# Layer-0 quantised network of a fused transformer kernel: bias by TensorE, gelu out of PSUM, scaling of the inner values on ScalarE, x updated in place

## The reference, cut to what matters

```python
def _layernorm(x, axis=-1, eps=1e-05):
    m = jnp.mean(x, axis=axis, keepdims=True)
    v = jnp.var(x, axis=axis, keepdims=True)
    return (x - m) / jnp.sqrt(v + eps)

def rmsnorm(x):
    return x * jax.lax.rsqrt(jnp.mean(x * x, axis=-1, keepdims=True) + EPS)
def act_quant(x):
    scale = 127.0 / jnp.clip(jnp.max(jnp.abs(x), axis=-1, keepdims=True), 1e-05)
    q = jnp.clip(jnp.round(x * scale), -128.0, 127.0) / scale
    return x + jax.lax.stop_gradient(q - x)
def weight_quant(w):
    scale = 1.0 / jnp.clip(jnp.mean(jnp.abs(w)), 1e-05)
    q = jnp.clip(jnp.round(w * scale), -1.0, 1.0) / scale
    return w + jax.lax.stop_gradient(q - w)
def bitlinear(x, w, b):
    xq = act_quant(rmsnorm(x))
    wq = weight_quant(w)
    return jnp.einsum('bsd,fd->bsf', xq, wq) + b

h = bitlinear(x, w1, b1)                      # 128 -> 512
h = jax.nn.gelu(h, approximate=False)
return bitlinear(h, w2, b2)                   # 512 -> 128
...
x = x + _L0_ffn_ref(_layernorm(x, axis=-1), L0_ffn_w1, L0_ffn_b1, L0_ffn_w2, L0_ffn_b2)
```

## Time and profile before

| what | us |
|---|---|
| median of 3 runs (lowest, highest) | 3688.69 (3678.2, 3689.1) |
| the profiled execution's own time | 3686.95 |
| its span in the profile | 3685.4 |
| start of the phase in the span (first weight load issued) | 188.62 |
| start of the next phase in the span | 494.41 |

### The profile page before, as it was taken

How to read it: one execution, slowest core, us unless ns; L and a number is a source line. 1 busy time by engine, 2 the same in 40 slices (tenths; PEclk the granted TensorE clock), 3 DMA queues, 4 the chain that set the end, 5 groups by cost and what they waited for, 6 DMA issues and landing times. The chain is left out here.

```text
span 3685.4 us, 67574 instructions
## 1 busy us (share of the span) xinstructions
PE 2706.8 (73%) x24298; PEld 1883.8 (51%) x24298; DVE 2401.7 (65%) x5736; ACT 1075.1 (29%) x1536; POOL 578.2 (16%) x1018
## 2 busy tenths in 40 slices
PE   5823359995999999999966677789850666886256
PEld 4612236663666565656545555556530554664126
DVE  6789969993455555555444688867013557988668
ACT  4533357761000000000022244445310112443230
POOL 0012210000000000000000144324133002443003
PEclk9955579997999999999977888889975777998669
DMA  2010011102221212121100000010221220000001
GB/s 82 23 55 0 0 33 30 27 13 92 92 78 61 91 48 92 46 92 46 46 25 18 8 1 0 0 37 27 89 65 38 60 60 11 0 0 7 0 0 46
DMA packets 119643, 141.77 MB, mean 38 GB/s; under 512 B 75745, under 2 KB 87649, under 8 KB 118498
## 3 DMA queue, kind: packets, MB, share of 16 engines
q1 hardware_dynamic: 112002, 119.85, 10.6%
q0 software_dynamic: 7520, 20.34, 1.9%
HBM read 122.85 MB, written 17.30 MB: 38 GB/s over the span
## 5 line engine op out<-in xcount | busy, mean ns | idle before, releaser
L1387 PE MATMUL banks<-l1f_xe,l1f_w 128*128 128x512 f32 x1024 | 486.2, 597 | 10.5 <-DVE l1f_xe L1586 10.5
L1586 DVE TENSOR_TENSOR l1f_xe<-l1f_hT,l1f_rwb 128x512 f32<-128x512 f32 x256 | 173.3, 692 | 300.3 <-PE banks L1389 278.1
L1389 PEld LDWEIGHTS banks<-l1f_w,l1f_xe 128*128 128x128 f32 x2048 | 270.0, 192 | 123.6 <-issue 123.6
L1592 DVE TENSOR_TENSOR l1f_ae<-l1f_aoT,l1f_rwb 128x512 f32<-128x512 f32 x256 | 172.7, 690 | 160.7 <-PE banks L1417 156.1
L1389 PE MATMUL banks<-l1f_w,l1f_xe 128*128 128x128 f32 x2048 | 270.7, 275 | 0.0
L1387 PEld LDWEIGHTS banks<-l1f_xe,l1f_w 128*128 128x128 f32 x1024 | 176.7, 192 | 140.9 <-issue 126.5
L1417 PE MATMUL banks<-l1f_ae,l1f_w 128*128 128x512 f32 x512 | 225.4, 599 | 1.4 <-DVE l1f_ae L1592 1.4
L214 POOL COPY x<-xn 128x512 f32 (+1 forms) x32 | 19.6, 611 | 986.4 <-DVE xn L1616 973.0
L223 PE MATMUL banks<-consts,l3p_h 128*128 128x128 f32 x64 | 17.8, 434 | 200.1 <-DVE l3p_h L140 200.1
L1417 PEld LDWEIGHTS banks<-l1f_ae,l1f_w 128*128 128x128 f32 x512 | 97.1, 192 | 118.3 <-issue 116.1
L612 PE MATMUL banks<-identb,l0f_q 128*128 128x128 bf16 x256 | 30.2, 312 | 129.0 <-DVE l0f_q L536 129.0
(11 more groups left out here) (471 smaller groups left out, 6651.1 us busy)
## 6 DMA issues: line engine op xcount, KB each, us to landing
l1f_rwb<-l1f_shares SPq DMA_DIRECT2D x128, 512.0 KB, 4.3
l1a_ctx<-in_ctxT SPq DMA_DIRECT2D x32, 256.0 KB, 3.7
l3p_ctx<-in_ctxT SPq DMA_DIRECT2D x32, 256.0 KB, 4.0
l0a_ctxT<-in_ctxT SPq DMA_DIRECT2D x16, 256.0 KB, 2.7
l2f_sent<-l0f_zero SPq DMA_DIRECT2D x4, 1024.0 KB, 7.8
l2p_ctxT<-in_ctxT SPq DMA_DIRECT2D x16, 256.0 KB, 2.7
...
```

The lines of the kernel that those rows point to most:

```text
L1387: pe.matmul(bank, w[:, n, e, :], xe[:, e % NB, :], start=(e == 0), stop=(e == E - 1))
L1389: last = pe.matmul(v_bank[:, D * j:D * j + D], xe[:, e % NB, P * j:P * j + P], w[:, 2, e, :], start=(e == 0 and j == 0), stop=(e == E - 1) ...
L1586: dve.tensor_tensor(xe[:, e % NB, :], hT[:, m, :], rwb[:, m, e, :], ALU.mult).then_inc(s.xe_ready, 1)
L1592: dve.tensor_tensor(ae[:, e % NB, :], aoT[:, m, :], rwb[:, m, e, :], ALU.mult).then_inc(s.ae_ready, 1)
```

## The change

`b1` is no longer spread over 128 partitions. It lies in four partitions, zero but for one row for each tile, and PE adds it: after the product of a tile, a second matmul with 4 rows of contraction, in f32, accumulates into the same bank. Its left side is `back`, the inverse of the token's step, transposed by PE (L589) and copied out by ACT (L631). So the bank holds (product + b1/step), and ACT's gelu reads each bank out of PSUM with the token's step as its scale, tile by tile. DVE's `bias` is gone. The multiplication of the inner values by the token's scale is four ACT Copies with a scale (`scale`). The clip to -128..127 is gone in both quantisations, so rounding writes bf16 itself. `new_x` adds in place into `k.x`, to which POOL has added b2 before (`add_bias`); `k.xb`, `k.xn` and the copy back are not used. The buffers of `h2` and of the small values have four places instead of two, and the loop body has four steps.

```diff
-def quantise_rows(dve, chain, q, h, scal, mean):
-
-
-    amax, r, inv, rec = scal[:, 0, :], scal[:, 1, :], scal[:, INV, :], scal[:, 6, :]
-    chain.wait(chain.did(dve.tensor_tensor(amax, amax, r, ALU.mult)))
-    chain.wait(chain.did(dve.tensor_scalar(amax, amax, 1e-5, None, ALU.max)))
-    chain.did(dve.tensor_scalar(inv, amax, mean, 1.0 / 127.0, ALU.mult, ALU.mult))
-    chain.wait(chain.did(dve.reciprocal(rec, amax)))
-    chain.wait(chain.did(dve.tensor_scalar(rec, rec, 127.0, None, ALU.mult)))
-    for j in range(TG):
-        n = chain.did(dve.tensor_scalar(h[:, j, :], h[:, j, :], r[:, j:j + 1], rec[:, j:j + 1], ALU.mult, ALU.mult))
-    chain.wait(n)
-    chain.wait(chain.did(dve.tensor_scalar(h, h, ROUND, ROUND, ALU.add, ALU.subtract)))
-    return dve.tensor_scalar(q, h, 127.0, -128.0, ALU.min, ALU.max)
...
+    RING4 = 4
...
-        b1 = sb("b1", [P, F0])
+        b1 = sb("b1", [TG, TG, F0])
...
+        hq = sb("hq", [P, TG, D])
+        sx = sb("sx", [P, RING4, 6, TG])
+        sh = sb("sh", [P, RING4, 8, TG])
...
+        back = sb("back", [TG, 2, P])
+        h2 = sb("h2", [P, RING4, TG, F0])
...
+        back_psum = ps[4][0:TG, GT // 2:GT // 2 + P]
+        AMAX, R, STEP, LEVELS, BACK, MEAN, POWER, FACTOR = range(8)
...
+            sp.wait_ge(s.cleared, 1)
+            for j in range(TG):
+                sp.dma_start(b1[j:j + 1, j, :], d["L0_ffn_b1"]).then_inc(s.b1_loaded, 16)
...
+            def turn_q(g, m):
                 pe.wait_ge(s.q_ready, g + 1)
                 wait(pe, s.qT_ready, g)
-                for j in range(TG):
-                    last = pe.transpose(psb[4][:, P * j:P * j + P], q[:, par, j, :], k.identb[:, :])
+                pe.transpose(back_psum, sx[:, m, BACK, :], k.ident)
+                for j in range(TG):
+                    last = pe.transpose(psb[4][:, P * j:P * j + P], q[:, m % 2, j, :], k.identb[:, :])
...
+            def up(g, m):
+
                 pe.wait_ge(s.qT_ready, g + 1)
-                wait(pe, s.h_ready, g)
-                for j in range(TG):
-                    last = pe.matmul(ps[j][:, :], qT[:, par, P * j:P * j + P], w1[:, :], start=True, stop=True)
-                last.then_inc(s.h_psum, 1)
-
-            def turn_q2(g, par):
+                for j in range(TG):
+                    wait(pe, s.gelu_ready, TG * (g - 1) + j + 1)
+                    pe.matmul(ps[j], qT[:, m % 2, P * j:P * j + P], w1[:, :], start=True, stop=False, skip_group_check=True)
+                    pe.matmul(ps[j], back[:, m % 2, :], b1[:, j, :], start=False, stop=True, skip_group_check=True).then_inc(s.h_psum, 1)
...
-            pipeline(pe, k.NG, [(1, up), (0, turn_q), (3, down), (2, turn_q2)])
+            pipeline(pe, k.NG, [(1, turn_q), (3, turn_q2), (1, up), (3, down)], unroll=RING4)
...
-            def copy_qT(g, par):
+            def copy_qT(g, m):
                 act.wait_ge(s.qT_psum, g + 1)
-                wait(act, s.h_psum, g - 1)
-                act.copy(qT[:, par, :], psb[4][:, 0:GT]).then_inc(s.qT_ready, 1)
-
-            def gelu(g, par):
-                act.wait_ge(s.h_ready, g + 1)
-                act.activation(h2[:, par].rearrange("p t f -> p (t f)"), h2[:, par].rearrange("p t f -> p (t f)"),
-                               ACT.Gelu).then_inc(s.gelu_ready, 1)
-                act.wait_ge(s.gelu_ready, g + 1)
...
+                act.copy(back[:, m % 2, :], back_psum)
+                act.copy(qT[:, m % 2, :], psb[4][:, 0:GT]).then_inc(s.qT_ready, 1)
+
+            def gelu(g, m):
+                wait(act, s.q2_ready, g - 3)
+                for j in range(TG):
+                    act.wait_ge(s.h_psum, TG * g + j + 1)
+                    act.activation(h2[:, m, j, :], ps[j], ACT.Gelu, scale=sx[:, m, STEP, j:j + 1]).then_inc(s.gelu_ready, 1)
...
+            def squares(g, m):
+                act.wait_ge(s.gelu_ready, TG * (g + 1))
                 wait(act, s.rms2_ready, g - 1)
                 for j in range(TG):
-
-                    last = act.activation(sq[:, par, j, :], h2[:, par, j, :], ACT.Square, scale=float(F0) ** -0.5, accum_out=scal[:, par, 2, j:j + 1])
+                    last = act.activation(sq[:, m % 2, j, :], h2[:, m, j, :], ACT.Square, scale=float(F0) ** -0.5,
+                                          accum_out=sh[:, m, MEAN, j:j + 1])
                 last.then_inc(s.rms2_arg, 1)
 
-            def copy_q2T(g, par):
+            def scale(g, m):
+                act.wait_ge(s.rr_ready, g + 1)
+                for j in range(TG):
+                    last = act.activation(h2[:, m, j, :], h2[:, m, j, :], ACT.Copy, scale=sh[:, m, FACTOR, j:j + 1])
+                last.then_inc(s.scaled, 1)
...
-            pipeline(act, k.NG, [(1, gelu), (0, copy_qT), (2, copy_q2T)])
+            pipeline(act, k.NG, [(1, copy_qT), (1, gelu), (3, copy_q2T), (2, scale), (1, squares)], unroll=RING4)
...
+            def add_bias(g, m):
+                pool.wait_ge(s.q_ready, g + 1)
+                settle(pool, k)
+                x = k.x[:, bass.ds(TG * g, TG), :]
+                pool.tensor_tensor(x, x, b2[:, :].unsqueeze(1).to_broadcast([P, TG, D]), ALU.add).then_inc(s.biased, 1)
...
-            pipeline(pool, k.NG, [(1, rms2), (2, lambda g, par: xb_pool(pool, k, s, g, par, b2)),
-                                  (3, lambda g, par: x_copy_pool(pool, k, s, g, par))])
...
+            def copy_mv(g, m):
+                pool.wait_ge(s.stats_ready, g + 1)
+                settle(pool, k)
+                pool.tensor_copy(k.mv[:, bass.ds(TG * g, TG), :], k.mvn[:, 0]).then_inc(s.mv_copied, 1)
+
+            pipeline(pool, k.NG, [(1, add_bias), (1, rms2), (4, copy_mv)], unroll=RING4)
...
+            def levels(chain, scal, mean):
+
+                amax, r, step, levels = (scal[:, n, :] for n in (AMAX, R, STEP, LEVELS))
+                chain.wait(chain.did(dve.tensor_tensor(amax, amax, r, ALU.mult)))
+                chain.wait(chain.did(dve.tensor_scalar(amax, amax, 1e-5, None, ALU.max)))
+                chain.did(dve.tensor_scalar(step, amax, mean, 1.0 / 127.0, ALU.mult, ALU.mult))
+                chain.wait(chain.did(dve.reciprocal(levels, amax)))
+                chain.wait(chain.did(dve.tensor_scalar(levels, levels, 127.0, None, ALU.mult)))
...
+                chain.did(dve.tensor_scalar(sx[:, m, BACK, :], sx[:, m, LEVELS, :], wsum[:, 4:5], None, ALU.mult))
+                for j in range(TG):
+                    n = chain.did(dve.tensor_scalar(hq[:, j, :], h[:, j, :], sx[:, m, R, j:j + 1], sx[:, m, LEVELS, j:j + 1], ALU.mult, ALU.mult))
+                chain.wait(n)
+                dve.tensor_scalar(q[:, m % 2], hq[:, :, :], ROUND, ROUND, ALU.add, ALU.subtract).then_inc(s.q_ready, 1)
...
-            pipeline(dve, k.NG, [(0, quantise_x), (1, bias), (2, quantise_h), (3, new_x)])
...
-            def bias(g, par):
-                dve.wait_ge(s.h_psum, g + 1)
-                wait(dve, s.q2_ready, g - 1)
-                for j in range(TG):
-                    last = dve.scalar_tensor_tensor(out=h2[:, par, j, :], in0=ps[j], scalar=scal1[:, par, INV, j:j + 1], in1=b1[:, :],
+            def levels_h(g, m):
+                chain = Chain(dve, s.b_chain, g, 7)
...
+                chain.did(dve.tensor_reduce(sh[:, m, AMAX, :], h2[:, m], AX_X, ALU.max, apply_absolute_value=True))
+                dve.wait_ge(s.rms2_ready, g + 1)
+                chain.did(dve.tensor_copy(sh[:, m, R, :], sh[:, m, POWER, :]))
+                chain.wait()
+                levels(chain, sh[:, m], wsum[:, 3:4])
+                dve.tensor_tensor(sh[:, m, FACTOR, :], sh[:, m, R, :], sh[:, m, LEVELS, :], ALU.mult).then_inc(s.rr_ready, 1)
+                chain.close()
+
+            def quantise_h(g, m):
+                dve.wait_ge(s.scaled, g + 1)
+                wait(dve, s.q2T_psum, g - 1)
+                dve.tensor_scalar(q2[:, m % 2], h2[:, m], ROUND, ROUND, ALU.add, ALU.subtract).then_inc(s.q2_ready, 1)
...
+            def new_x(g, m):
+                chain = Chain(dve, s.stats_chain, g, TG)
+                dve.wait_ge(s.y_psum, g + 1)
+                dve.wait_ge(s.biased, g + 1)
+                settle(dve, k)
+                for j in range(TG):
+                    x = k.x[:, bass.ds(TG * g + j, 1), :]
+                    last = dve.scalar_tensor_tensor(out=x, in0=ps[7][:, D * j:D * j + D], scalar=sh[:, m, STEP, j:j + 1], in1=x,
...
+                wait(dve, s.mv_copied, g)
+                dve.memset(k.pad[:, :], 0.0)
...
+            pipeline(dve, k.NG, [(4, new_x), (2, levels_h), (0, quantise_x), (2, quantise_h)], unroll=RING4)
...
-    lay["L0_ffn_b1"] = rows(a["L0_ffn_b1"])
+    lay["L0_ffn_b1"] = a["L0_ffn_b1"][None, :]
```

More of the change, by code:

```diff
@@ L744, in _ @@
-            pipeline(dve, k.NG, [(0, quantise_x), (1, bias), (2, quantise_h), (3, new_x)])
+                last.then_inc(s.xn_ready, 1)
+                dve.wait_ge(s.xn_ready, g + 1)
+                settle(dve, k)
+                for j in range(TG):
```

(6 more changed lines are left out.)

68 lines of the change are left out of this document (27 added, 41 removed).

## The result

The changed kernel takes 3704.2 us (median of 5 runs, 3698.3 to 3709.3) where the kernel before takes 3687.55 (median of 5, 3678.2 to 3689.1) on the same chip: a ratio of 1.005, 95% interval 1.0032 to 1.0067. It is slower by half a per cent; forecast were 3643 us and 1.2% faster. Its profiled execution took 3701.49 us with a span of 3699.9.

What follows compares the result with a forecast made beforehand. DVE bound the kernel before; afterwards ACT with PE's tiles would: 8.63 + 5.65 = 14.3 us, 14.4 with POOL's queue. Fourteen such rounds plus edges saved 44 us: 3686.95 - 44 = 3643, own range 3634 to 3652, whole range 3620 to 3666.

Steps and rivals of the forecast that it cites:

- The step that failed: PE's burst of q2 transposes (1.7 us) and four tiles: clock rises inside, one tile slow, three fast, 5.65 us in all.
- no row shows so few rows for long: Rival: products with 4 rows don't raise the clock; tiles 8.8 us, round 17.5, 3690 us, no change; chance 0.07.
- the slower one: Rival: lower clock throughout plus uncovered weight loads, 0.28 us more a tile; tile 2.5, round 18.6, 3708 us; chance 0.05.
- The weight loads: PE's loads at each tile: no cost in the forecast sum, 0.28 us a tile only in the slower rival.
- DVE's round: DVE's work per group after the change: 12.4 us, with 5.7 us a group taken off.
- ACT's round without PE: ACT's copies, last gelu, scalings and squares per group, without PE's four tiles: 8.63 us.
- The round: Loop time per group: ACT with PE's tiles 14.3 us, plus 0.1 for POOL's queue, 14.4 us.
- POOL's queue: Wait for POOL's statistics copy behind rms2: 0.1 us a round; as the bound, a rival at 15.2 a round, 3654, chance 0.10.
- POOL's power: POOL's power in rms2, moved beside new_x: the shared-port rule would favour the short price, 1.06 us against 2.39.
- The edge: Phase start: b1's row loads and POOL's clearing of b1 run beside DVE's preparation; nothing, or 2 us if cover fails.
- The sum: Whole phase: start, fourteen rounds of 14.4 us and drain, 44.7 us saved, taken as 44, giving 3643 us.
- The rival of the later rise: Rival: PE's clock rises a tile later, two slow tiles, 1.05 us more a round, 3658 us; chance 0.13.

Runs made afterwards that it cites:

- rows128: Changed kernel with the f32 bias product over 128 rows of contraction instead of 4, 124 of them zero: 3642.5 us, 0.985 of the kernel before.
- rows96: Changed kernel with the f32 bias product over 96 rows of contraction instead of 4, 92 of them zero: 3631.4 us in one run.
- scale_dve: Changed kernel with the four multiplications of the inner values back on DVE instead of ACT: 3658.6 us, 0.989 of the kernel before.

## Why the prediction was wrong

**The step that failed** is the sentence "A burst of 1.7 + 8.8 us will see the clock rise inside it", and with it the term 5.65 us for PE's four tiles. Measured: 4 x 2.54 = 10.2 us. The working took one hard fact, that bursts of products raise the clock, from bursts of products that all had 128 rows of contraction (the one row with few, L2398 in the earlier trace rows, shows two records and no rise), and carried it to a burst of which two thirds are products with 4 rows. It even named the gap, in a rival ("no row shows so few rows for long"), and gave it 0.07. A property that no row showed, and on which 47 us hung by that rival and 65 by the slower one, deserved a chance near even. The runs with 96 and 128 rows show the term itself well made for products with all rows: 2.10 + 3 x 1.07 = 5.3 us.

**The weight loads**, 0.44 us a tile (2.54 less 2.10), were priced at nothing in the sum and stood only in the slower rival, as 0.28 a tile. Of the 4.8 us a round between the changed kernel and `rows128` they make some 1.8 (4 x 0.44) and the clock some 3.1 (3 x (2.10 - 1.07)). That rival (tile 2.5, round 18.6, 3708 us) is what happened: tile 2.54, round 18.4, 3704 us. It had 0.05. That its tile fits so well is in part luck: it put 2.2 for a tile without bare loads, which takes 2.10, and 0.28 for loads that take 0.44.

**DVE's round** of 12.4 us: it could not show in the changed kernel, as DVE waits 5.3 us for ACT's scaling and 0.95 for POOL, but 18.4 minus 5.3 minus 0.95 is 12.15. Right to 0.25.

**ACT's round without PE**, 8.63: measured 18.4 - 10.2 = 8.2, the copy of back 0.24, the gelu behind the last tile 0.69, the scalings 2.57 with 2.46 from start to the squares. Right to 0.4.

**The round** for a clock that rises inside the burst, 14.4: with 128 rows it is 13.6. The difference is 0.4 from ACT, 0.35 from the tiles and the 0.1 for POOL's queue, which was not needed.

**POOL's power** took 1.03 us in the new place and not 2.39. The prediction expected that from the rule on the shared port pair, which the Trainium skill gives on the page "SBUF — State Buffer", section "Who interferes with whom". The trace has the short price but does not test the rule as the prediction applied it: the power (347.96 to 348.99) did not run beside new_x, which had ended at 347.31, but beside 0.4 us of the statistics and then a DVE that waited for POOL.

**The edge** failed a little: POOL now clears `b1` (1.79 us) ahead of the zeros (1.79), and DVE's first operation of the phase, beside them, takes 3.55 instead of 1.81. The timeline of the changed kernel, POOL and DVE:

```profile
189.12 1.79 POOL L665 MEMSET l0f_b<- 4x2048 f32 x1 [0.92 <-POOLq L114]
190.87 1.79 POOL L666 MEMSET l0f_zero<- 128x2048 f32 x1
...
189.17 3.55 DVE L130 TENSOR_SCALAR rstd<-mean_var 128x64 f32<-128x64 f32 x1 [1.31 <-PEq L114]
```

Before, the clearing of the zeros ran from 188.62 to 190.42 and DVE's operation ended at 190.48; now the second memset ends at 192.66 and DVE's at 192.72. In every run it ends some 0.05 us behind the end of one of POOL's memsets, but not always the last: with the three of `rows128` it took 1.81 and ended behind the first, with the three of `rows96` 2.06, behind the second. Which one lets it through stays open. The first q is ready 1.0 us later than before, 0.5 of it because the phase itself begins later; the 2 us given for a cover that fails enclose it.

**The sum.** In the changed kernel DVE's reductions of the inner values lie 278.4 us apart from the first to the sixteenth, before 255.2. With rounds of 13.6 (`rows128`) the phase is 56.9 us shorter than before, where 44 were forecast; 14 times the 0.8 us a round makes 11 of the difference.

**The rival of the later rise** (3658) is not borne out: with 96 and 128 rows one tile was slow, and in `scale_dve` the clock rose inside sixteen transposes. The Trainium skill, page "TensorE: Matmul & The Clock Gate", section "Part 4: PE-mode transpose", says that transposes do not count as busy in the same way, by which it would have come later; these runs give that no support.
